# Attention with 16 heads of dimension 8: fp32 scores in two row groups instead of bf16 pieces through a DRAM scratch

## The reference

```python
h = layernorm(x)                                    # (4, 256, 128)
q, k, v = h @ Wq + bq, ctx @ Wk + bk, ctx @ Wv + bv
s = q.heads @ k.heads.T * 8 ** -0.5 + bias[a]       # (4, 16, 256, 256)
s = s + mask                                        # a: 0, 1, 2, each with its own bias
o = softmax(s) @ v.heads
x = x + tanh(gate[a]) * (o.merge @ Wo + bo)
```

## Time and profile before

| | |
|---|---|
| median of 3 runs | 860.76 us (860.72 to 862.41) |
| profiled execution | 862.37 us, span 860.4 |
| mean granted TensorE clock | 0.898 of full |
| PE, DVE, ACT, POOL busy | 702.3, 573.1, 488.9, 166.6 us |
| attention 0: first min run, last residual | 43.85, 138.14 |
| attention 1: first min run, last residual | 181.52, 275.69 |
| attention 2: first min run, last residual | 472.36, 566.18 |

### The profile page before, as it was taken

One profiled execution on the slowest core, in us unless ns is written; L12 is line 12 of the kernel. 1 busy time (PEld: TensorE's weight loads), 2 busy tenths in 40 slices (PEclk: granted clock), 3 DMA queues, 4 the chain that ended last, 5 costly groups with the idle time before them and its releaser, 6 DMA issues. The chain is left out here.

```text
span 860.4 us, 14382 instructions
## 1 busy us (share of the span) xinstructions
PE 702.3 (82%) x4728; PEld 396.0 (46%) x4728; DVE 573.1 (67%) x1765; ACT 488.9 (57%) x1323; POOL 166.6 (19%) x135
## 2 busy tenths in 40 slices
PE   4589994559997878999744899949999999869978
PEld 2266663336665323333222667635336666644322
DVE  3699995869996358667865999855316666436553
ACT  2288881259883568598812988812666556413201
POOL 8622000420000045536655000020000000000000
PEclk8689997769999768998885999979999999969999
DMA  8895004060000000000009200000000000000000
GB/s 310 169 319 177 2 7 69 23 126 2 2 2 2 0 1 0 1 0 1 1 0 180 41 2 2 2 26 0 1 0 1 1 2 2 1 1 1 0 1 24
DMA packets 22056, 32.26 MB, mean 38 GB/s; under 512 B 1760, under 2 KB 15712, under 8 KB 21216
## 3 DMA queue, kind: packets, MB, share of 16 engines
q1 hardware_dynamic: 21984, 31.36, 14.4%
HBM read 21.39 MB, written 9.96 MB: 36 GB/s over the span
## 5 line engine op out<-in xcount | busy, mean ns | idle before, releaser
L816 ACT ACTIVATE RING<-RING,NMX 128x256 f32<-128x256 f32 x384 | 190.7, 500 | 56.2 <-DVE NMX L1637 55.8
L1637 DVE CUSTOM_DVE_ANT_0 RING<-bank,ADJM 128x256 f32<-128x256 f32 x384 | 143.4, 413 | 23.5 <-DMA scratch<-RING 22.5
L1158 PE MATMUL bank<-W,RING 128*128 128x128 f32 x768 | 120.5, 282 | 15.6 <-ACT RING L828 13.9
L541 POOL TENSOR_TENSOR small<-small 128x8 f32<-128x8 f32 (+2 forms) x13 | 17.7, 1365 | 463.1 <-DVE small L1528 463.1
L1158 PEld LDWEIGHTS bank<-W,RING 128*128 128x128 f32 x768 | 91.7, 145 | 27.9 <-ACT RING L816 23.2
L1138 PE MATMUL bank<-ARENA 128*128 128x256 bf16 x384 | 77.8, 290 | 30.7 <-DMA ARENA<-scratch 25.7
L1649 DVE COPY RING<-bank 128x512 f32<-128x512 f32 x144 | 98.6, 686 | 1.2 <-PE bank L1158 0.8
L816 ACT ACTIVATION_READ_ACCUMULATOR RING<-RING,NMX 128x1 f32 x384 | 72.8, 190 | 0.0
L997 PE MATMUL bank<-XT,W 128*128 128x512 f32 (+2 forms) x118 | 62.2, 668 | 6.6 <-ACT XT L712 5.3
L728 ACT ACTIVATE RING<-bank,NMX 128x512 f32<-128x512 f32 x64 | 43.4, 683 | 41.8 <-PE bank L1062 21.2
L1280 PE MATMUL bank<-ARENA,W 64*128 64x512 f32 x180 | 62.3, 710 | 3.6 <-DVE ARENA L1830 2.3
(11 more groups left out here) (253 smaller groups left out, 1307.3 us busy)
## 6 DMA issues: line engine op xcount, KB each, us to landing
scratch<-ARENA SPq DMA_DIRECT2D x18, 256.0 KB, 3.2
ARENA<-scratch SPq DMA_DIRECT2D x6, 768.0 KB, 10.6
W<-in_weights SPq DMA_DIRECT2D x1, 2564.0 KB, 21.2
scratch<-RING SPq DMA_DIRECT2D x36, 64.0 KB, 3.0
ARENA<-scratch SPq DMA_DIRECT2D x12, 192.0 KB, 3.8
scratch<-RING SPq DMA_DIRECT2D x18, 128.0 KB, 2.9
ARENA<-scratch SPq DMA_DIRECT2D x6, 384.0 KB, 6.6
W<-in_weights SPq DMA_DIRECT2D x2, 1024.0 KB, 13.7
```

The lines of the kernel that those rows point to most:

```text
L816: nc.scalar.activation(P_OF(n)[:, q * S:(q + 1) * S], S_OF(n)[:, q, :], ACT.Exp, bias=NMX[:, 2 * t + q:2 * t + q + 1], scale=-1.0, accum_o ...
L1158: mm = nc.tensor.transpose(bk[:, o:o + P], P_OF(n)[:, i:i + P], ident)
L1637: nc.vector.tensor_tensor_reduce(out=S_OF(n)[:, q, :], in0=SBANK(n)[:, q * S:(q + 1) * S], in1=ADJM[:, b, q, :], scale=-1.0, scalar=BIG, o ...
```

## The change

**What it does.** The bf16 split, the scratch and the large memsets go. Queries and keys stay fp32: head j of four stands on 8 rows from row 32j of QT and KT (four groups g). The first batch's are made in place by matmuls in four column groups (heads); the rest is computed compactly (QC, KC) and scattered by SP in 16 transfers of 8 partitions each (scatter). compact(a) loads 16 pieces of Wo so that the projection needs one matmul per tile.

A unit is now two heads and one query tile: two fp32 matmuls with 8 rows in row groups 2jj and 2jj + 1, into banks 2jj and 2jj + 1 (banks 0 to 3), the next unit with jj changed; its score waits for the min run of unit n − 2. The transposed units use two banks (4, 5), and are copied by DVE (even units) and ACT (odd). V has a column of ones per head, so P·V also gives the sums; OTR is copied by DVE, transposed back (ONE_T, L1211 in the changed kernel), divided there (L1654's and L1659's work on tiles 128x8 and 128x64), transposed (BACK_T, L1220) and projected (OUT_T, L1231, L1232). In the loop stand also: later_queries at t = 1, values at t = 3 (a = 0, 2), out_row at t = 5 (a = 0), and other_masks on DVE at t = 6 (a = 0). keys(1), keys(2), values(1) and the rows out_row(1), out_row(2) stand between attentions 0 and 1. POOL makes half of the next masks earlier and clears 1344 columns only. On ACT the exponentials write no sums, the copy of odd units has the form of the DVE one, and at BACK_T it copies the turned outputs (OTN2).

The core of the diff (lines removed are those of the functions above, and mostly left out):

```diff
-LAG, PV_T, OTR_T, SEL_T, OUT_T = 3, 8, 9, 13, 27
-PT_SLOTS = 7
+LAG, PV_T, OTR_T, ONE_T, BACK_T, OUT_T, END_T = 3, 7, 9, 11, 25, 29, 14
 PIECES = [(0, S), (S, 2 * S), (2 * S, 4 * S)]
-QK_AT = [2, 9, 12]
+PITCH = DH + 1
+LATER = [(S, 3 * S), (3 * S, 4 * S)]
...
-        QS = ARENA[:, 0:8192].bitcast(BF16).rearrange("p (h t) -> p h t", h=H16)
-        KS = ARENA[:, 8192:12288].bitcast(BF16).rearrange("p (j t) -> p j t", j=H16 // 2)
+        QT = ARENA[:, 0:4096].rearrange("p (g t) -> p g t", g=4)
+        KT = ARENA[:, 4096:8192].rearrange("p (g t) -> p g t", g=4)
+        PT = ARENA[:, 8192:12288].rearrange("p (s j k q) -> p s j k q", s=2, j=4, k=2)
         V = ARENA[:, 14336:14336 + NT * VW].rearrange("p (t f) -> p t f", t=NT)
...
+        QC = ARENA[:, 17216:18240]
+        KC = [ARENA[:, 18240:19264], ARENA[:, 19264:20288], w("wk0", 0, TOK)]
+        WOC = [ARENA[:, 20288:20416], ARENA[:, 12288:12416], w("wk1")]
...
+            sp.dma_start(ADJ[:, 0, :, :], adj_in[:, 0, :, :]).then_inc(s_ldm, 16)
+            sp.dma_start(MASK[:, 0, :, :], mask_in[:, 0, :, :]).then_inc(s_ldm, 16)
+            sp.dma_start(MASK[:, 1:B, :, :], mask_in[:, 1:B, :, :]).then_inc(s_ldm2, 16)
+            sp.dma_start(PADW[:, :], pad_in).then_inc(s_ldm2, 16)
...
+            def scatter(dst, src, t0, done):
+                for g in range(NG):
+                    for j in range(HG):
+                        r = PAD * g + DH * j
+                        sp.dma_start(dst[PAD * j:PAD * j + DH, g, t0:TOK], src[r:r + DH, t0:TOK]).then_inc(done[g], 16)
+            compact(0)
+            sp.wait_ge(s_he, NG + 2)
+            scatter(KT, KC[0], S, s_ks)
+            sp.wait_ge(s_ea, QC_AT[0])
+            scatter(QT, QC, S, [s_qs] * NG)
+            sp.dma_start(ADJ[:, 1:3, :, :], adj_in[:, 1:3, :, :]).then_inc(s_ldm2, 16)
...
+                for t in range(UNITS + END_T):
...
+                        n, m, jj = base + t, t // 2, t % 2
+                        b, g, q = m // 8, m // 2 % 4, m % 2
...
+                        if t == 16:
+                            pe.wait_ge(s_qs, 16 * H16 * (a + 1))
+                            if a == 0:
+                                for k in range(NG):
+                                    pe.wait_ge(s_ks[k], 16 * HG)
...
+                        else:
+                            pe.wait_ge(s_max, 2 * n - 2)
+                        for j in (2 * jj, 2 * jj + 1):
+                            r = slice(PAD * j, PAD * j + DH)
+                            mm = nc.tensor.matmul(bank[j][:, 0:S], QT[r, g, b * S + q * P:b * S + (q + 1) * P],
+                                                  KT[r, g, b * S:(b + 1) * S], start=True, stop=True)
                         mm.then_inc(s_s, 1)
+                    if t == 1:
+                        later_queries(a)
+                    if a != 1 and t == 3:
+                        values(a, ra, s_fa)
+                    if a == 0 and t == 5:
+                        out_row(0, ra, s_fa)
                     u = t - LAG
                     if 0 <= u < UNITS:
                         n = base + u
                         pe.wait_ge(s_exp, 2 * n + 2)
...
+                            pe.wait_ge(s_te if n % 2 else s_to, n // 2)
                         bk = TBANK(n)
+                        for i in range(4):
+                            mm = nc.tensor.transpose(bk[:, i * P:(i + 1) * P], P_OF(n)[:, i * P:(i + 1) * P], ident)
                         mm.then_inc(s_t, 1)
                     k = t - PV_T
+                    if k >= 0 and k % 2 == 0 and k // 4 < UNITS // 4:
+                        G, part = k // 4, k % 4 // 2
                         GG = base // 4 + G
                         b, g = G // 4, G % 4
                         if part == 0:
+                            pe.wait_ge(s_te, 2 * GG + 2)
+                            pe.wait_ge(s_to, 2 * GG + 2)
+                            pe.wait_ge(s_otr, GG)
...
+                        for j in range(HG):
+                            f = PITCH * (HG * g + j)
+                            mm = nc.tensor.matmul(bank[6][PAD * j:PAD * j + PAD, 0:S], V[:, 2 * b + part, f:f + PAD],
+                                                  PT[:, GG % 2, j, part, :], start=(part == 0), stop=(part == 1))
                         if part == 1:
+                            mm.then_inc(s_pv, 1)
+                    if t >= ONE_T and (t - ONE_T) % 4 == 0 and (t - ONE_T) // 4 < UNITS // 4:
+                        G = (t - ONE_T) // 4
+                        GG, b = base // 4 + G, B * a + G // 4
+                        pe.wait_ge(s_otr, GG + 1)
+                        pe.wait_ge(s_on, GG)
...
+                        for q in range(TPB):
+                            mm = nc.tensor.transpose(bank[7][:, q * P:(q + 1) * P],
+                                                     OTR[:, GG % 2, q * P:(q + 1) * P], ident)
+                        mm.then_inc(s_one, 1)
...
+                        pe.wait_ge(s_on, 4 * i + 4)
+                        for q in range(TPB):
+                            mm = nc.tensor.transpose(bank[7][:, q * P:(q + 1) * P], ON[:, i % 2, q, :], ident)
+                        mm.then_inc(s_back2, 1)
                     if t >= OUT_T and (t - OUT_T) % 16 == 0:
...
+                        i = B * a + b
+                        pe.wait_ge(s_otn, i + 1)
+                        pe.wait_ge(s_on, min(4 * i + 5, 16 * a + 16))
...
                         for q in range(TPB):
+                            o = bank[7][:, q * P:(q + 1) * P]
+                            nc.tensor.matmul(o, OTN2[:, i % 2, q * P:(q + 1) * P], WOC[a], start=True, stop=False)
+                            mm = nc.tensor.matmul(o, ones_row, BOR[a], start=False, stop=True)
+                        mm.then_inc(s_o, 1)
...
+            def other_masks():
+                dve.wait_ge(s_ldm2, 48)
+                mask_terms(1, B)
...
+                        n, m, jj = base + t, t // 2, t % 2
+                        b, q = m // 8, m % 2
+                        if a == 0 and t == 6:
+                            other_masks()
...
+                        for i in range(2):
                             nc.vector.tensor_tensor_reduce(
+                                out=S_OF(n)[:, i, :], in0=bank[2 * jj + i][:, 0:S],
                                 in1=ADJM[:, b, q, :], scale=-1.0, scalar=BIG, op0=ALU.add, op1=ALU.min,
+                                accum_out=NMX[:, 2 * t + i:2 * t + i + 1]).then_inc(s_max, 1)
                     u = t - LAG
+                    if 0 <= u < UNITS and u % 2 == 0:
                         n = base + u
...
+                    if t >= OTR_T and (t - OTR_T) % 4 == 0 and (t - OTR_T) // 4 < UNITS // 4:
+                        GG = base // 4 + (t - OTR_T) // 4
+                        dve.wait_ge(s_pv, GG + 1)
...
+                        nc.vector.tensor_copy(OTR[:, GG % 2, :], bank[6][:, 0:S]).then_inc(s_otr, 1)
+                    if t >= ONE_T and (t - ONE_T) % 4 == 0 and (t - ONE_T) // 4 < UNITS // 4:
...
+                        dve.wait_ge(s_one, GG + 1)
...
+                        src = bank[7][:, 0:S].rearrange("p (q j r) -> p q j r", q=2, j=HG)
+                        link(nc.vector.reciprocal(RS, src[:, :, :, DH:PITCH]))
+                        nc.vector.tensor_tensor(
+                            ON[:, i % 2, :, PAD * g:PAD * g + PAD].rearrange("p q (j d) -> p q j d", j=HG),
+                            src[:, :, :, 0:DH], RS.to_broadcast([P, TPB, HG, DH]), ALU.mult).then_inc(s_on, 1)
```

More of the change, by code:

```diff
@@ L30 @@
 PW = NG * P
-VW = H16 * DH + PAD - DH
+VW = 168
 NE = 8
@@ L376, in program @@
         l_o, l_x = sem("l_o"), sem("l_x")
-        scratch = [nc.dram_tensor(f"scratch{i}", (H16 * 6 * DH, TOK), BF16, kind="Internal").ap() for i in range(6)]
         block = stack.enter_context(nc.Block())
@@ L473, in write @@
-            def write(side, parts, slots, cut, ready, n_ready, written):
-                rows = scratch[side].rearrange("(h i d) t -> i h d t", h=H16, i=6)
-                for part in range(3):
-                    sp.wait_ge(ready, n_ready + part + 1)
-                    for i in slots[part]:
-                        sp.dma_start(rows[i][:, :, cut], parts[:, part, cut]).then_inc(written, 16)
-            def read(side, dst, cut, written, n_written, done):
-                sp.wait_ge(written, n_written)
-                rows = scratch[side].rearrange("(j e r) t -> e r j t", e=2, r=6 * DH)
-                for e in range(2):
-                    sp.dma_start(dst(e)[:, :, cut], rows[e][:, :, cut]).then_inc(done, 16)
@@ L545, in roots, with masks @@
                 root(TPB, NT)
-            def masks(a):
+            def masks(a, b0, b1):
                 if a > 0:
                     pool.wait_ge(s_max, 2 * UNITS * a)
-                for b in range(B):
+                for b in range(b0, b1):
                     for q in range(TPB):
@@ L609, in _ @@
```

(52 more changed lines are left out.)

491 lines of the change are left out of this document (208 added, 283 removed).

## The result

| | before | after |
|---|---|---|
| median | 860.86 us | 1107.98 us (1102.3 to 1115.94, 4 runs) |
| ratio, 95% interval | | 1.287 (1.279 to 1.295) |
| profiled execution, span | 862.37, 860.4 | 1107.31, 1105.5 |
| mean granted clock | 0.898 | 0.717 |
| attention 0, first min run to end of last residual | 43.85 to 138.75 | 21.22 to 229.89 |

The page of the changed kernel, its first lines: busy us (share), and PE's busy tenths and granted clock in 40 slices.

The account below looks back on a forecast made before the run. DVE was taken to bound the old loop (5.34 us per four units), PE the new (6.8). Attentions +9, +14.5 and +6.7, together +30, gave 892 against 862.4, 890 beside the median; 8-in-10 range 838 to 976.

Parts of the forecast that it names:

- rival 2: Attention 0 stays at 1.2 GHz after PE's stop at unit 6: .18 at about 972, .07 beyond 1000.
- the PE's stop is built in: Argument for the slow-clock rival: PE stops some 10 us at unit 6 of attention 0, waiting on DVE's masks.
- full-row transposes and P·V are still most of the work: Argument against the slow-clock rival: the new loop's work is mostly full-row, as in old loops whose clock rose.
- 1050 to 1150: Total in us if attentions 1 or 2 are caught at 1.2 GHz too; .07 for beyond 1000.
- The price at .50: Loop at 1.2 GHz: streaming 9.5 and shape changes about 2.7, 12.2 us per four units.
- The price at 1.00: Loop at full clock: 4.76 work + 1.78 shape changes + .3 wait, 6.8 us per four units.
- The changes of shape: PE's loop: 11 tile-shape changes per four units instead of 4, at .20, .15 or .12 each, 1.78 us.
- P·V's wait: In the loop PE waits for ACT's copy ahead of P·V, 2.8 against 2.3 us of work: about .3 per four units.
- the likeliest case: PE-bound loop at full clock, total 872 to 905 us, chance .42.
- The prologues: Ahead of the loops: attention 0's first min about 21 instead of 43.85; attention 1 saves 10 us, attention 2 19.5.
- Unit 6: Attention 0: DVE waits for the ADJ load, then makes masks for 4.4 us; this min at about 40 (39 to 44).
- rival 3: The two row groups run one after the other: +1.71 us per four units, total 968; chance .05.

Follow-up runs that it names:

- e12: Against the changed kernel: early load of ADJ[:,1:3] and other_masks ahead of the loop, still 8 rows per head; 1108.84 us.
- e2: Against the changed kernel: each score matmul uses all 32 rows of its row group instead of 8, output not the reference's; 982.91 us.
- e9: Against e5: other_masks stands ahead of the loop instead of at unit 6, still 32 rows per head; 911.92 us.
- e6: Against the changed kernel: two units' scores issued together, four heads in four row groups, 8 rows per head, early ADJ load; 953.28 us.
- e11: Against the fast version (four heads side by side, 32 rows, dense schedule, 817.65 us): rows back to 8 per head; 821.94 us.
- e5: Against the changed kernel: 32 rows per head with zeroed key rows and the reference's output, early ADJ load; 971.5 us (2 runs).
- e4: Against the changed kernel: two unneeded bf16 matmuls of 128 rows and 512 columns ahead of each unit's transposes; 962.35 us.

## Why the prediction was wrong

- **The step that failed** is in rival 2, "the PE's stop is built in" on one side and "full-row transposes and P·V are still most of the work" on the other. I treated the fall as something that only a stop causes, gave attention 0 alone .18 and more loops .07. The loop as written, with 8 rows per head, doesn't hold 2.4 GHz (e12, and attention 1 of the changed kernel after 31 us), so all three were caught: the case "1050 to 1150" came true. The rows had a hint: at 312 to 316 PE was busy 4.00 of 4.00 at .50 with 64-row and 24-row work. I used it only for rising, not for holding. What I set against it was misread too: by the terms of the sum, transposes are 1.71 of the old loop's 4.28 us of work, 40% and not two thirds, and of the new loop's 6.8 us full-row transposes and P·V are less than half.
- **The price at .50 was right**: 12.2 per four units forecast, 12.25 measured, though in part by luck: the projection costs .8 of it where it was counted at .54, and the rest 11.45 where it was 11.7. With it, the prediction's own terms give 890 + 82 + 90 + 90 = 1152 for three cold loops. The measured 1108 is less in part because attention 1 ran 31 us at 1.00; 17 units at 1.18 less each are 20 us (an estimate from 7.5 against 12.25 per four).
- **The price at 1.00** was 6.8 forecast and 30.2 / 4 = 7.5 measured with projection (e2). The changes of shape came to 1.9 per four units against 1.78: by the starts above, .20 to .21 from the row pair into the full array, .16 out of it (into the pair or into P·V's column groups), .14 to .15 behind P·V and L1211. P·V's wait was .63 instead of .3; the prediction's own 2.8 against 2.3 us give .5, so the .3 didn't follow from them. The projection and its surroundings were .46 per four units instead of .27. The direction didn't hang on the clock: e9, with every loop at 1.00 but for the dip at its start, is at 911.92, slower than before by 51, and above the 872 to 905 of the likeliest case.
- **The prologues**: first min at 21.22 against "about 21"; attention 1 10.7 less against 10; attention 2 20.9 less against 19.5. Unit 6 came at 46.14, not at 40. The 32 scatters took 22.07 us, .69 each against the .63 of the row, so that the ADJ load went out at 37.80 rather than 35; DVE went on 3.75 us later, and the masks took 4.6 instead of 4.4. The forecast's own 35, 3.0 and 4.4 add up to 42.4 and not 40.
- **DVE and ACT** were off the critical path, as forecast; rival 3 (row groups one after the other) is out by the starts of L1161.
- **Drain at a change of tile mode**: the Trainium skill, "TensorEngine Tiling (Array Packing)", Key Properties, agrees with these gaps, .14 to .21 at each change. They explain 1.9 us of each four units and not the 247 us. That transposes don't count for the clock in the same way as other matmuls (the Trainium skill, "TensorE: Matmul & The Clock Gate", Part 4) didn't keep e9's loop down, which holds 1.00 with a quarter of its time in transposes; no run here isolates them.

## What to carry to other kernels

Shrinking a matmul's contraction to few rows can cost more than its own time: here TensorE's clock fell for most of each loop, and then all of PE's work took longer, four units 11.45 us instead of 7.08. Read the granted clock per loop beside PE's busy share, and where it is .50 with PE full, test it by padding with zero rows, by filler, or by putting small matmuls side by side in all row groups, which here also removed 4 of the 11 changes of shape. Take PE's short waits out with it (e6 against e11). Keep slow work of another engine out of a loop on which PE waits.

## What the hardware did that I hadn't expected

- The same loop can run at either clock for its whole length. With 32 rows it held 1.00 for 102 us (e9) and stayed at .50 for 160 us when 4.6 us of mask work had stopped PE at unit 6 (e5): 60 us of total time by one order of instructions. In e9 the same mask work came ahead of the loop and the clock fell too, at 25 us, but it was back at 32, while PE made the values; in e5 the values were done before the stop. That they are what brought it back is likely and not shown by a run of its own.
- Work that nobody needs made the kernel 13% faster (e4, 962.35 against 1107.98), since the clock came back.
- PE busy at 160.00 of 160.00 us is not a sign of an engine at full clock: in the changed kernel these are the stretches at .50, while at 1.00 its loop was busy 27.09 of 30.00. In e4 100.00 of 100.00 us were at 1.00, so that the busy share says nothing of the clock by itself.
